# Moving the first norm and the weight splits into the block of the first attention

## What is computed

```python
x = x + jnp.tanh(g_xattn[0]) * _L0_xattn_ref(_layernorm(x, axis=-1), ctx_1024, L0_xattn_Wq, L0_xattn_Wk, L0_xattn_Wv, L0_xattn_Wo, L0_xattn_bo)
...
    q = (x @ Wq).reshape(b, n, H, DH)
    k = (context @ Wk * SCALE).reshape(b, m, H, DH)
    v = (context @ Wv).reshape(b, m, H, DH)
    scores = jnp.einsum('bihd,bjhd->bhij', q, k)
    attn = jax.nn.softmax(scores, axis=-1)
    out = jnp.einsum('bhij,bjhd->bihd', attn, v)
    return out @ Wo + bo
```

## Time and profile before

| | us |
|---|---|
| median of 3 runs (1683.59 to 1685.87) | 1683.79 |
| the profiled execution: its own time | 1687.02 |
| its span in the trace | 1685.3 |
| TensorE busy in the span | 1414.1 (84%) |
| VectorE busy | 1234.5 (73%) |
| ScalarE busy | 1110.6 (66%) |
| GpSimd busy | 214.3 (13%) |

### The profile page before, as it was taken

How to read it: one execution, slowest core, us unless ns; L and a number is a source line. 1 busy time by engine, 2 the same in 40 slices (tenths; PEclk the granted TensorE clock), 3 DMA queues, 4 the chain that set the end, 5 groups by cost and what they waited for, 6 DMA issues and landing times. The chain is left out here.

```text
span 1685.3 us, 40493 instructions
## 1 busy us (share of the span) xinstructions
PE 1414.1 (84%) x15436; PEld 1006.3 (60%) x15436; DVE 1234.5 (73%) x3090; ACT 1110.6 (66%) x2449; POOL 214.3 (13%) x189
## 2 busy tenths in 40 slices
PE   1799999999999994492456989898989869999996
PEld 1466666776666663340443666666666647788884
DVE  6478888878888877768764888898988877434443
ACT  5467777777777773467324888888888744366663
POOL 4401000000000001200014000000000010034443
PEclk9999999999999997696676999999999769999998
DMA  4122322223333211000011212120100053222231
GB/s 143 56 70 89 106 94 95 82 83 106 98 97 95 86 51 63 1 0 1 1 40 49 79 44 83 42 83 18 33 21 21 7 181 121 63 40 46 46 49 23
DMA packets 64910, 105.69 MB, mean 63 GB/s; under 512 B 7433, under 2 KB 38898, under 8 KB 63570
## 3 DMA queue, kind: packets, MB, share of 16 engines
q1 hardware_dynamic: 58002, 94.83, 17.8%
q0 software_dynamic: 6720, 8.27, 3.0%
HBM read 68.88 MB, written 35.11 MB: 62 GB/s over the span
## 5 line engine op out<-in xcount | busy, mean ns | idle before, releaser
L1279 ACT ACTIVATE a_p<-a_s,a_nb 112x375 f32<-112x375 f32 x256 | 140.9, 598 | 27.9 <-DVE a_nb L1380 27.2
L294 PE MATMUL a_ps_o<-a_vh,a_pt 125*128 125x64 f16 (+1 forms) x1536 | 153.1, 183 | 3.0 <-ACT a_pt L1292 0.8
L1204 PE MATMUL a_ps_t<-ident,a_p 112*128 112x112 f32 x768 | 119.8, 288 | 40.3 <-ACT a_p L1279 39.4
L296 PE MATMUL a_ps_o<-a_vh,a_pt 125*128 125x64 f16 (+1 forms) x1536 | 151.3, 182 | 0.0
L295 PE MATMUL a_ps_o<-a_vl,a_pt 125*128 125x64 f16 (+1 forms) x1536 | 151.1, 182 | 0.0
L583 ACT ACTIVATE a_p<-a_ps_s,a_nb 112x375 f32<-112x375 f32 x256 | 143.8, 573 | 3.4 <-DVE a_scaled L674 3.4
L591 ACT ACTIVATE a_pt<-a_ps_t 125x336 f16<-125x336 f32 x256 | 101.7, 448 | 66.1 <-PE a_ps_t L522 65.7
L294 PEld LDWEIGHTS a_ps_o<-a_vh,a_pt 125*128 125x128 f16 x1536 | 133.7, 98 | 15.9 <-ACT a_pt L1292 7.5
L1204 PEld LDWEIGHTS a_ps_t<-ident,a_p 112*128 112x128 f32 x768 | 81.4, 148 | 95.7 <-issue 80.5
L295 PEld LDWEIGHTS a_ps_o<-a_vl,a_pt 125*128 125x128 f16 x1536 | 131.1, 98 | 11.2 <-issue 0.3
L1371 DVE TENSOR_TENSOR a_s<-a_ps_s,a_mask 112x750 f32<-112x750 f32 x128 | 119.6, 935 | 20.3 <-PE a_ps_s L1194 16.3
(11 more groups left out here) (365 smaller groups left out, 4536.6 us busy)
## 6 DMA issues: line engine op xcount, KB each, us to landing
a_piece<-in_w SPq DMA_DIRECT2D x72, 256.0 KB, 3.1
split_weights<-a_pair SPq DMA_DIRECT2D x72, 256.0 KB, 3.4
w<-split_weights SPq DMA_DIRECT2D x8, 1024.0 KB, 5.8
a_ctx<-in_ctxT SPq DMA_DIRECT2D x16, 375.0 KB, 3.7
ctx<-a_cx SPq DMA_DIRECT2D x16, 375.0 KB, 4.4
a_cx<-ctx SPq DMA_DIRECT2D x16, 375.0 KB, 5.3
w1h<-split_weights SPq DMA_DIRECT2D x2, 1792.0 KB, 14.0
w1l<-split_weights SPq DMA_DIRECT2D x2, 1792.0 KB, 16.2
```

Source lines behind the costliest of these rows:

```text
L294: nc.tensor.matmul(out, wh, mh, start=(i == 0), stop=False)
L296: last = nc.tensor.matmul(out, wl, mh, start=False, stop=(i == n - 1))
L1204: mm = nc.tensor.matmul(ps_t[:, 2 * (g % 2) + i, t * S:(t + 1) * S], p32[:, g % 2, i, t * KV:t * KV + 128], ident32[0:S, 0:S], start=(t == ...
L1279: nc.scalar.activation(p32[:, g % 2, i, 0:NC], s2[:, g % 2, i, :], ACT.Exp, bias=nb[:, g % 2, i:i + 1], scale=-1.0).then_inc(exp_done, 1)
```

## The change

The two blocks ahead of the attention's block are gone. Their work is written into its code:

- SP loads the context of batch 0 first, then Wk, four batches of x, Wq, the gates, Wv, bias, the other twelve batches of x, Wo. There are four weight stages.
- ScalarE makes the high half of a weight in one pass with the scale; VectorE, not GpSimd, makes the low half, again from the stage.
- `FIRST` holds all K and Q jobs of batch 0, and two new jobs X0 and X1, which transpose a group of four normalised batches (k half 0 and 1). `JOBS_0` is shorter by that.
- Statistics of the other twelve batches are taken in slots 3 to 5, their root in slot 6, the steps to the reciprocal root in slot 7. The groups are normalised in slot 1 of batches 1, 4 and 8 and transposed by X jobs in slots 3 and 4 of these batches. Wo is split in slots 1 and 2.
- The bias is added batch by batch on GpSimd between its casts of the context.

```diff
-def setup_phase(nc, A, x_res, ident32, ident16, gates, x_in, g_in):
...
-            sp.dma_start(x_res[:], A["x"].rearrange("(t p) d -> p t d", p=S)).then_inc(x_in, 16)
...
+        WK, WQ, WV, WO = ((2 * n, 2 * n + 1) for n in range(4))
+        SB = 4
+        stage = sb("a0_stage", [128, SB, IN0])
+        xn = sb("a0_xn", [S, TG, D])
+        stats, mv = sb("a0_stats", [S, B, 6]), sb("a0_mv", [S, B, 2])
+        var, std, rstd, near = (sb(f"a0_{n}", [S, B]) for n in ("var", "std", "rstd", "near"))
...
-        norm_phase(nc, "n0", x_res, ident32, xh, xl, start=start, weights=([
...
-        FIRST = [("Q0", 0), ("K0", 0), ("K1", 0)]
-        JOBS_0 = [[("V00", 0), ("K2", 0)], [("V01", 0), ("V02", 0), ("K3", 0)], [("K4", 0), ("Q1", 0)],
-                  [("K5", 0), ("V10", 0)], [("V11", 0), ("K6", 0)], [("V12", 0), ("K7", 0)],
-                  [("OT0", 0), ("Q0", 1), ("K0", 1), ("K1", 1)],
-                  [("K2", 1), ("K3", 1), ("Q1", 1), ("K4", 1), ("K5", 1), ("K6", 1)]]
+        FIRST = [("K0", 0), ("K1", 0), ("K2", 0), ("K3", 0), ("X0", 0), ("X1", 0), ("K4", 0), ("K5", 0), ("Q0", 0),
+                 ("Q1", 0), ("K6", 0), ("K7", 0)]
+        JOBS_0 = [[("V00", 0)], [("V01", 0), ("V02", 0)], [("V10", 0), ("V11", 0)], [("V12", 0), ("K0", 1)],
+                  [("K1", 1), ("Q0", 1)], [("K2", 1), ("K3", 1)], [("OT0", 0), ("Q1", 1), ("K4", 1)],
+                  [("K5", 1), ("K6", 1)]]
+        GROUP_AT = {1: 1, 4: 2, 8: 3}
...
+            js = [(n, b + off) for n, off in JOBS[p] if b + off < B]
+            if b in GROUP_AT and p in (3, 4):
+                js.append((f"X{p - 3}", GROUP_AT[b]))
+            return js
...
+            def load_weight(i):
+                src, hi, lo = loads[i]
+                wait(sp, w_lo, i - (SB - 1))
+                sp.dma_start(stage[:, i % SB, 0:hi.free_size()].rearrange("p (a b) -> p a b", a=src.shape[1]),
+                             src).then_inc(w_in[i % SB], 16)
+            def load_rows(t0, t1, landed):
+                sp.dma_start(x_res[:, t0:t1, :], A["x"].rearrange("(t p) d -> p t d", p=S)[:, t0:t1, :]
+                             ).then_inc(landed, 16)
             sp.dma_start(ctx32[:], A["ctxT"][:, :, 0:NC].rearrange("k p n -> p k n")).then_inc(ctx_in, 16)
+            for i in WK:
+                load_weight(i)
...
+            load_rows(0, TG, x_in[0])
+            for i in WQ:
+                load_weight(i)
+            for i, name in enumerate(("g_xattn", "g_ffn")):
+                sp.dma_start(gates[:, 2 * i:2 * i + 2], A[name].partition_broadcast(128)).then_inc(g_in, 16)
+            for i in WV:
+                load_weight(i)
             sp.dma_start(bo[:], A["L0_xattn_bo"].partition_broadcast(S)).then_inc(bo_in, 16)
             sp.dma_start(nw[:], A["norm_wT"]).then_inc(nw_in, 16)
+            load_rows(TG, B, x_in[1])
+            for i in WO:
+                load_weight(i)
...
+                if (name, b) == ("K0", 0):
+                    pe.wait_ge(w_lo, WK[1] + 1)
+                if (name, b) == ("Q0", 0):
+                    pe.wait_ge(w_lo, WQ[1] + 1)
+                    pe.wait_ge(job_lo, NUMBER["X1", 0] + 1)
+                if (name, b) == ("V00", 0):
+                    pe.wait_ge(w_lo, WV[1] + 1)
+                if (name, b) == ("W", 0):
+                    pe.wait_ge(w_lo, WO[1] + 1)
+                if name == "Q0" and b % TG == 0 and b > 0 and NUMBER["X1", b // TG] + 1 > i - 1:
+                    pe.wait_ge(job_lo, NUMBER["X1", b // TG] + 1)
+                if name == "X0":
+                    pe.wait_ge(normed, TG * (b + 1))
+                if (name, b) == ("X0", 0):
+                    pe.wait_ge(id_made, 2)
...
-            pe.wait_ge(zeroed, 4)
             for name, b in FIRST:
                 job(name, b)
+            pe.wait_ge(zeroed, 4)
...
+            def weight_high(i):
+                src, hi, lo = loads[i]
+                act.wait_ge(w_in[i % SB], 16 * (i // SB + 1))
+                nc.scalar.activation(hi, stage[:, i % SB, 0:hi.free_size()], ACT.Copy, scale=WS).then_inc(w_hi, 1)
+            def roots(n, t0, t1):
+                act.wait_ge(var_ready, n)
+                nc.scalar.activation(std[:, t0:t1], var[:, t0:t1], ACT.Sqrt).then_inc(std_ready, 1)
             act.wait_ge(ctx_in, 16)
             nc.scalar.activation(cx[:, 0, 0, :, :], ctx32[:], ACT.Copy).then_inc(ctx_hi, 1)
+            for i in WK:
+                weight_high(i)
+            high("K0", 0)
+            roots(1, 0, TG)
+            high("K1", 0)
+            for i in WQ:
+                weight_high(i)
+            high("K2", 0)
+            high("K3", 0)
+            act.wait_ge(g_in, 32)
+            nc.scalar.activation(tanh_g[:], gates[:], ACT.Tanh).then_inc(tanh_done, 1)
+            act.wait_ge(zeroed, 4)
+            for name, b in FIRST[4:]:
+                high(name, b)
+            for i in WV:
+                weight_high(i)
...
+                if g in (1, 2):
+                    weight_high(WO[g - 1])
+                if g == 6:
+                    roots(2, TG, B)
...
-            pool.wait_ge(bo_scaled, 1)
-            for b in range(B):
+            def add_bias(b):
+                pool.wait_ge(normed, TG * (b // TG + 1))
                 nc.gpsimd.tensor_tensor(x_res[:, b, :], x_res[:, b, :], bo_g[:], ALU.add).then_inc(bo_added, 1)
             for b in range(1, B):
                 c = b % 2
+                if b == 2:
+                    pool.wait_ge(bo_scaled, 1)
+                if b >= 2:
+                    add_bias(b - 2)
...
+                    dve.wait_ge(bo_added, b + 1)
...
+            def weight_low(i):
+                src, hi, lo = loads[i]
+                dve.wait_ge(w_hi, i + 1)
+                nc.vector.scalar_tensor_tensor(out=lo, in0=stage[:, i % SB, 0:hi.free_size()], scalar=WS, in1=hi,
+                                               op0=ALU.mult, op1=ALU.subtract).then_inc(w_lo, 1)
...
+            for i in WK:
+                weight_low(i)
+            dve.wait_ge(x_in[0], 16)
+            stat(statistics(0, TG))
+            variances(0, TG)
+            low("K0", 0)
+            reciprocal_roots(1, 0, TG)
+            normalise_rows(0)
+            low("K1", 0)
+            for i in WQ:
+                weight_low(i)
+            low("K2", 0)
+            low("K3", 0)
+            dve.wait_ge(zeroed, 4)
+            for name, b in FIRST[4:]:
+                low(name, b)
+            for i in WV:
+                weight_low(i)
             dve.wait_ge(bo_in, 16)
+            dve.wait_ge(tanh_done, 1)
             nc.vector.tensor_scalar(bo_g[:], bo[:], tanh_g[0:S, 0:1], None, ALU.mult).then_inc(bo_scaled, 1)
             link(nc.vector.tensor_scalar(gate[:], tanh_g[0:S, 0:1], 1.0 / (WS * WS), None, ALU.mult))
-            dve.wait_ge(zeroed, 4)
-            for name, b in FIRST:
-                low(name, b)
-            dve.wait_ge(bo_added, B)
...
+                if g in (1, 2):
+                    weight_low(WO[g - 1])
+                if g == 3:
+                    dve.wait_ge(x_in[1], 16)
+                if 3 <= g < 6:
+                    last = statistics(TG * (g - 2), TG * (g - 1))
+                if g == 5:
+                    stat(last)
+                    variances(TG, B)
+                if g == 7:
+                    reciprocal_roots(2, TG, B)
+                if g % NP == 1 and g // NP in GROUP_AT:
+                    normalise_rows(GROUP_AT[g // NP])
```

91 lines of the change are left out of this document (58 added, 33 removed).

## The result

The changed kernel takes 1674.97 us (median of 4 runs, 1673.10 to 1675.79), the kernel before 1684.44 (4 runs on the same chip): a ratio of 0.9943, with an interval of 0.993 to 0.9956, 9.5 us faster. The forecast was 1662, so the sign was right and the gain less than half of the forecast 22.

What follows compares the result with a forecast made beforehand. The head was taken as bound by latency, the slots by TensorE's work. Gains of 25.6 us by slot 8, less 2.7 and 1.0, made 22: span 1663.3, profiled time 1665, less 3.2 gives 1662, range 1652 to 1670.

Steps and rivals of the forecast that it cites:

- The head: Start up to slot 1's scores: K0 at 9.4, scores at 38.4 against 61.78, 23.4 us earlier.
- Slots 1 to 7: First batch up to slot 8's scores: 36.7 us including stalls, slot 8 at 75.1, 25.6 earlier.
- A slot's own price: TensorE's scores, transposes and weighted values in each slot: 1.84 us, from a batch of 35.9 less 21.2 of jobs.
- The half clock: TensorE in slots 1 to 7: 2.4 us extra for 4.8 us at half clock.
- The stalls: Slots 1 to 7: 4.9 us from VectorE's added work and ScalarE's table loads, bounds 0 and 11.2.
- Behind slot 8: Later batches: X jobs lose 2.7 and normalisations 1.0, leaving 22 us of the 25.6 gained.
- six X jobs: TensorE after slot 8: 0.45 us each, 2.7 lost, since TensorE is full there.
- the next slot has room: VectorE's normalisations at slots 9, 33 and 65: 1.35 us each, only 0.3 each showing, 1.0 in all.
- The subtraction of 3.2: Whole kernel: the median lies 3.2 us below the profiled execution's own time, taking 1665 to 1662.
- VectorE becomes the bound of the first batch: First batch: all extras show, 11.2 instead of 4.9, head at half clock to K7; gain 12, 1672; chance 0.18.
- Less is lost: Full clock over the gap before V00, stalls 1 instead of 4.9 in slots; gain 30, 1654; chance 0.13.
- Slower: Half clock through all of slots 1 to 7: 5 us slower, 1689; chance 0.03.

Runs made afterwards that it cites:

- x first: The changed kernel with all 16 batches of x asked for ahead of the context and Wk, as in the kernel before: 1680.24 us.
- X behind: The changed kernel with X0's high half moved behind the exponentials on ScalarE in slots 11, 35 and 67: 1667.68 us.
- both: The changed kernel with one normalisation in each of the first four slots of batches 1, 4, 8 and X jobs in the fifth and sixth: 1662.38 us.
- statistics spread: "both" with statistics two batches per slot in slots 2 to 7, second root in slot 8, rows and X jobs a slot later: 1663.52 us.
- exp table early: The changed kernel plus a one-column Exp right behind the second root, to load the table of Exp there: 1672.78 us.
- best: "both" plus Wv split behind K4 and K5, statistics in slots 2 to 5, aggregates in 6, second root in 7, reciprocal steps in 8: 1656.92 us.

## Why the prediction was right in sign and wrong in size

**The head, right.** Forecast and measured: K0 at 9.4 and 10.47 (9.4 to 10.6 in the later traces but for "x first"; Wk's second piece was split from 8.01, not 7.1); Wv's low halves done at 34.0 and 35.5; slot 1's scores at 38.4 and 38.94. K0 and K1 at half clock: the matmuls are 0.31 apart for all of K0 and half of K1, up to 13.24. PEclk reads 1.00 in that stretch; its first fall stands at 20.1, so the distances are the better sign there. V00 ran at the full clock in the first trace, which made good 1.3 of the 1.5 by which Wv was late. In nine of the ten later traces of the changed head the half clock came after all: in four of them ("X behind", "both", "statistics spread", "exp table early") V00's matmuls are 0.43 apart, as forecast, and in five it came at the end of V00 or behind it. The normalisations took 0.33 each in the head, as taken from the earlier trace rows. The mean of 0.90 in the old head hid two kinds: eleven of the sixteen took 0.40 (0.33 from start to start) and five took 2.2, each of which started within 0.2 us behind the start of a GpSimd subtraction of 2.1 to 2.3 us (L228).

**Slots 1 to 7, right in sum, with two small errors that cancel.** 36.7 forecast, 35.85 measured. By the forecast's own prices the jobs of these slots (5 V, 7 K, 2 Q, 1 OT) are 15.95, not 16.5. A slot's own price was too small: the 538.6 between the first and the last residual addition was divided by 15, but its last two intervals, where the pipeline drains, are 35.4 and 25.6, and a steady batch is 36.74. So the price is (36.74 - 21.2)/8 = 1.94 and not 1.84, 0.7 more in seven slots. TensorE needs 15.95 + 13.6 = 29.55, where 29.4 was forecast. The half clock cost 1.3 (in slot 7), where 2.4 was forecast; in the later traces it cost 1.6 to 2.2, in slot 1, and nothing in "best". The stalls are 35.85 - 29.55 - 1.3 = 5.0, where 4.9 was forecast. Of these, 2.0 are VectorE's work of slot 5, seen in slot 6 (6.81, in "statistics spread" 4.78; "about 2" forecast), 1.7 the table loads (2.2 forecast), and 1.3 the rest (0.7 forecast).

**Behind slot 8, wrong: this is the failed step.** The prediction said there: "six X jobs at 0.45 on TensorE, which is full there, 2.7 lost", and of the normalisations "the next slot has room, 0.3 each, 1.0"; so three batches "about 1 longer". They were 3.5 to 5.1 longer. The first figure was near: 2.1 where the X jobs stood, 2.6 in "both". The second was 2.9. And a term was missing: I looked at TensorE and VectorE for these slots and not at ScalarE's order. In slots 11, 35 and 67 the evacuation of X0 stands ahead of the exponentials while X0 is TensorE's last job, 1.8 each, 5.4 in all. With the stretch at half clock behind one such gap (1.65) it makes 12.1 instead of 3.7.

**The rest.** 0.9 went in the drain, whose last 17 us had a granted clock of 0.81 (0.90 before), and 1.6 behind the attention. The forecast put both at nothing: it let everything behind the first attention move as a block. The sum: 25.9 - 12.1 - 0.9 - 1.6 = 11.3, against 22 forecast. The subtraction of 3.2 from the profiled time to the median was too much by 2.4: after's own profiled time is 1675.79, 0.8 above its median.

**The rivals.** The gain came out at that of "VectorE becomes the bound of the first batch" (12), but not by its mechanism: the first batch gave what was forecast, and the loss lay in batches 1, 4 and 8. Of "Less is lost" one half came, by luck of the run: V00 was at the full clock behind the gap of 3.42 in five of the nine traces that have this gap. Its other half, stalls of 1, did not. "Slower", half clock through the slots, did not come: apart from short stretches the slots stayed at 2.4 GHz.

## What to carry to other kernels

When a job is added to slots of a hand-written pipeline, write down its place in the queue of every engine that touches it, not only its cost: the loss was largest where TensorE's last job of a slot was ScalarE's first. A rule such as "the first job ahead of the exponentials" has to be read with the list as it stands after its filter. Four short operations on a queue that is 80% busy are free one per slot and cost 0.97 us when they stand together.

## What the runs showed of the hardware

- Leaving out a root between exponentials, and with it both table loads, gave 1.7 us (slot 7 at 5.75 or 4.02). Both loads side by side cost as much as apart (5.84).
- A gap of 1.7 us on TensorE in an otherwise full stretch was followed by a fall of the granted clock in 9 of 21 slots with the same order of instructions, at 1.65 us each; gaps of 1.6 to 2.0 in batch 0 were followed by one once in 17. Two traces of one kernel differ in which slots it hits, so a difference of 1 to 2 us between two traces is to be looked for in the clock first.
- In the kernel before, five of sixteen normalisations on VectorE took 2.2 us instead of 0.40, each started just behind a GpSimd subtraction of 2.1 to 2.3 us.
- Slots without such a fall repeat to 0.01 us between runs and between kernels, far better than the medians (0.2%), as long as their work and their neighbours are the same. The effect of an edit inside the pipeline is best read from slot lengths.
